# Alternating chunks of the convolution and of the projection two units ahead, on TensorE and ScalarE

## What is computed

```python
qkv = jnp.einsum('oc,bchw->bohw', w_qkv, x)                 # the projection
y = conv_general_dilated(qkv, w_dw, (1, 1), [(2, 2), (2, 2)],
                         feature_group_count=3 * INNER)     # 5x5 depthwise
agg = jnp.einsum('gok,bgkhw->bgohw', w_pw, y_grouped)        # 8x8 pointwise, by group
qkv_ms = concatenate([qkv, agg], axis=1)
# per head of 8: q, k = relu(q), relu(k); v1 = [v, 1]
vk = einsum('bhdn,bhen->bhde', v1, k)
out = einsum('bhde,bhen->bhdn', vk, q); out = out[:-1] / (out[-1:] + EPS)
out = einsum('oc,bchw->bohw', w_proj, out)                   # then batch norm, + x
```

## Time and profile before

| | |
|---|---|
| median of 3 runs | 2769.11 us (2768.99 to 2770.96) |
| the profiled execution | 2770.3 us, span 2768.5 us |
| TensorE busy | 2478.3 us, 90% of the span |
| VectorE busy | 2246.0 us, 81% |
| ScalarE busy | 870.1 us, 31% |
| mean granted TensorE clock | 0.955 of full |

### The profile page before, as it was taken

One profiled execution on the slowest core, in us unless ns is written; L12 is line 12 of the kernel. 1 busy time (PEld: TensorE's weight loads), 2 busy tenths in 40 slices (PEclk: granted clock), 3 DMA queues, 4 the chain that ended last, 5 costly groups with the idle time before them and its releaser, 6 DMA issues. The chain is left out here.

```text
span 2768.5 us, 42532 instructions
## 1 busy us (share of the span) xinstructions
PE 2478.3 (90%) x16192; PEld 1546.5 (56%) x16192; DVE 2246.0 (81%) x1677; ACT 870.1 (31%) x1685; POOL 316.9 (11%) x206
## 2 busy tenths in 40 slices
PE   7999999995998999899999999999999999999740
PEld 6888888883444554555455454555545554554420
DVE  5666666775999999899889979998997999999452
ACT  4444443442233233222323232232323233232241
POOL 2222222211000010100001010101000010100000
PEclk9999999997999999999999999999999999999975
DMA  2111110006787478477947757694776669576758
GB/s 90 69 69 69 70 69 36 35 35 191 161 181 175 103 157 206 90 169 161 217 93 161 181 118 166 137 219 98 159 181 145 136 138 217 114 160 146 246 210 372
DMA packets 89625, 397.89 MB, mean 144 GB/s; under 512 B 26480, under 2 KB 27120, under 8 KB 83696
## 3 DMA queue, kind: packets, MB, share of 16 engines
q1 hardware_dynamic: 88304, 376.43, 54.5%
q0 software_dynamic: 1152, 18.87, 1.6%
HBM read 75.12 MB, written 54.26 MB: 47 GB/s over the span
## 5 line engine op out<-in xcount | busy, mean ns | idle before, releaser
L1054 DVE SCALAR_TENSOR_TENSOR work<-work,dws 128x2304 f32<-128x2304 f32 x576 | 1511.9, 2625 | 19.5
L675 PE MATMUL cv<-work,w 128*32 128x384 f32 x6912 | 625.6, 495 | 17.8 <-ACT q L947 12.7
L653 PE MATMUL pj<-x,wqkv 128*128 128x384 f32 x1152 | 387.6, 488 | 20.4 <-DMA x<-scratch_x 20.4
L675 PEld LDWEIGHTS cv<-work,w 128*32 128x32 f32 x6912 | 195.7, 110 | 361.8 <-issue 330.0
L653 PEld LDWEIGHTS pj<-x,wqkv 128*128 128x128 f32 x1152 | 214.7, 191 | 158.6 <-issue 23.3
L680 PE MATMUL cv<-work,pwbd 128*128 128x384 f32 x576 | 266.4, 545 | 26.3 <-DVE work L1054 26.3
L897 ACT ACTIVATE work<-cv 128x384 f32<-128x384 f32 x192 | 94.5, 492 | 508.7 <-PE cv L680 508.7
L1012 POOL TENSOR_TENSOR vkm<-vkraw,mask 128x128 f32<-128x128 f32 x32 | 45.3, 1415 | 1652.5 <-ACT vkraw L917 1652.5
L872 ACT COPY work<-pj 128x384 f32<-128x384 f32 x288 | 139.0, 482 | 271.5 <-PE pj L653 243.1
L696 PE MATMUL vk<-kvT 128*128 128x129 f32 x1216 | 198.6, 286 | 8.9 <-ACT kvT L910 6.0
L680 PEld LDWEIGHTS cv<-work,pwbd 128*128 128x128 f32 x576 | 86.6, 190 | 207.8 <-issue 170.0
(11 more groups left out here) (108 smaller groups left out, 3304.6 us busy)
## 6 DMA issues: line engine op xcount, KB each, us to landing
work<-work SPq DMA_DIRECT2D x1536, 169.0 KB, 3.7
x<-scratch_x SPq DMA_DIRECT2D x9, 2304.0 KB, 10.5
scratch_x<-xs SPq DMA_DIRECT2D x8, 2304.0 KB, 7.2
xs<-in_x SPq DMA_DIRECT2D x7, 2304.0 KB, 8.6
scratch_y<-q SPq DMA_DIRECT2D x21, 768.0 KB, 3.8
work<-scratch_y SPq DMA_DIRECT2D x5, 2304.0 KB, 29.5
out<-work POOLq DMA_DIRECT2D x5, 2304.0 KB, 14.5
work<-scratch_x SPq DMA_DIRECT2D x4, 2304.0 KB, 32.0
```

The lines of the kernel that those rows point to most:

```text
L653: mm = nc.tensor.matmul(pj[:, c % 2, :CHUNK], wqkv[:, kc, u, :], x1[:, kc, c * CHUNK:(c + 1) * CHUNK], start=(kc == 0), stop=(kc == CT - 1))
L675: nc.tensor.matmul(cv[32 * b:32 * b + 32, c % 2, :CHUNK], w4[:, 4 * u + b, dy, :], taps[:, row + dy:row + dy + 8, 0:W], start=(dy == 0), s ...
L1054: op = nc.vector.scalar_tensor_tensor(out=a, in0=src, scalar=w, in1=a, op0=ALU.mult, op1=ALU.add)
```

## The change

In `image` of TensorE (L809) and of ScalarE (L957), for every unit but unit 2, a chunk of the projection two units ahead is issued right after the chunk of the convolution with the same number, inside the first loop of the unit. In the second loop it is left for unit 2 only. No instruction is added or removed, and no wait is changed; SyncE, GpSimd and VectorE keep their queues.

```diff
@@ TensorE, and the same in ScalarE @@
                     for c in range(NCH):
                         convolve(i, u, [c])
+                        if u != 2 and (u + 2 < NU or nxt):
+                            project(*unit_at(i, u + 2), [c])
                         if u == 2:
                             product(i, 2, shares(DG)[c])
                         if u == 5:
                             product(i, 3, shares(AG)[c])
                     if u == 4:
                         turn_product(i, 2)
                     for c in range(NCH):
-                        if u + 2 < NU or nxt:
+                        if u == 2:
                             project(*unit_at(i, u + 2), [c])
                         if u == 1:
                             product(i, 1, shares(AG)[c])
```

## The result

| | before | after |
|---|---|---|
| median | 2770.03 us (4 runs, 2768.99 to 2775.0) | 2907.9 us (4 runs, 2903.09 to 2912.76) |
| ratio to before | | 1.0494, 95% interval 1.0472 to 1.0516 |
| span of the profiled execution | 2768.5 us | 2911.0 us |
| mean granted TensorE clock | 0.955 | 0.935 |

The change makes the kernel 4.9% slower. The page still shows both large engines' busy time nearly unchanged: what has grown is waiting.

What follows compares the result with a forecast made beforehand. TensorE, by its own queue, was taken to bound the looped images. Terms of 20.2 us per looped image, 121 us for six, plus 14 in image 0, made 135 us: 2905 on the profiled 2770.3, median 2904, range 2848 to 2938.

Steps and rivals of the forecast that it cites:

- The bound: Looped images: TensorE's own queue sets the pace; its idling is paid in full, what reaches VectorE earlier is worth nothing.
- The alternation is free: Units 0, 1, 3, 4 and 5: convolution, projection, convolution costs 4.21 us, the same as the two apart.
- Product 1: Unit 1: loses its cover, only the first group's copy, some 0.3 us, can't be hidden; taken as 0, -0.2 to +0.5.
- `x1` in unit 4: Unit 4: TensorE's projection waits for the next image's input, 7.7 us, grown to 9.0 us, between 7.5 and 10.5.
- the tail of the `rep` loads: Unit 4: these loads land until some 39.5 us and delay `x1` by up to 1.9 us of shared transfer.
- The clock: Behind each of the two new TensorE waits, coming back from half clock costs 2.1 us (1.7 to 2.6).
- The end of unit 4: `turn_product` loses the projection ahead of it; waiting for ScalarE's copy, with the transpose, costs 0.85 us.
- half 0 of `rep`: Start of unit 5: this load is just in time for ScalarE's chunk 0 of the projection, 0.1 us.
- ScalarE's wait in unit 5: ScalarE's projection chunk 0 waits for half 1 of `rep`; TensorE idles 4.7 us, with backlog about 5.0 (3.5 to 6).
- The end of unit 5: `turn_product` waits for GpSimd's mask of the last product, which the projection covered before: 1.05 us.
- Image 0: First image, with slack for some of the loss: 5.4 us, and unit 5 adds 8.2, 14 us in all.
- The sum: 20.2 us per looped image, 121 us for images 1 to 6, with image 0 together 135 us.

Runs made afterwards that it cites:

- e1: The changed kernel with chunks alternating in units 0, 1 and 3 alone, units 4 and 5 as before: 2772.93 us, 1.0015 of the kernel before.
- e2: The changed kernel with chunks alternating in unit 4 alone: 2847.68 us, 1.0282 of the kernel before.
- e5: The changed kernel with ScalarE waiting for half 1 of `rep` only ahead of chunk 2, not chunk 0: 2860.04 us, 1.0334 of the kernel before.
- e4: The changed kernel with SyncE's load of the next `x1` moved between the two halves of unit 4's `rep` loads: 2871.44 us, 1.0371 of the kernel before.
- e6: The changed kernel with both `x1` loaded sooner and ScalarE's wait for `rep` split: 2826.77 us, 1.0214 of the kernel before.
- e9: As e6, but ScalarE itself issues the store of output chunks 4 and 5: 2807.86 us, 1.014 of the kernel before.
- e7: The kernel before with TensorE's loop over images 1 to 6 written out: 2740.45 us, 0.9907 of the kernel before.
- e3: The changed kernel with chunks alternating in unit 5 alone: 2809.3 us, 1.0143 of the kernel before.

## Why the prediction was right

The forecast was 2904 us, the measured median 2907.9. By its own steps:

- **The bound.** TensorE sets the pace, and VectorE's readiness is worth nothing: right. TensorE waits for no tap in any looped image, before or after, and what is new in its waits is paid in full.
- **The alternation is free:** right, 4.21 us per pair in e1. The Trainium skill's rule in "TensorEngine Tiling (Array Packing)", Key Properties, that a change of tiling mode drains TensorE, can't be told apart from its absence here, since the count of changes is the same in both orders.
- **Product 1:** taken at 0, range to 0.5; measured 0.7 per image, outside that range. Of it 0.42 us is the wait for the first group's copy (I had said 0.3); the rest is spread over the groups, a few hundredths each.
- **`x1` in unit 4:** 9.0 us forecast, 7.4 to 8.9 measured, 7.9 on average. Right mechanism. I had given the tail of the `rep` loads 1.3 us; comparing 7.9 with the 6.6 of e2, where unit 3 doesn't alternate, gives the shared tail this very 1.3, though no run varied the tail alone. It was the base of 7.7 us that was too high: I had taken the median landing of 10.5 us, and in e2 TensorE resumes 9.56 us after the issue (1594.85 to 1604.41).
- **The clock:** 2.1 us for each wait, and too low. The 2.07 of the image shown is near it by chance. In the six looped images the pair that resumes behind `x1` takes 5.93 to 7.30 us against 4.21, which is 1.7 to 3.1 us and 2.5 on average; in e2 it is 2.6. Behind the wait of unit 5, TensorE goes from chunk 1 to chunk 3 in 11.13 us where it doesn't wait (e5) and in 16.9 to 18.6 in the changed kernel. Less its waits, that leaves 1.6 to 3.1 us, 2.4 on average.
- **The end of unit 4:** 0.85 forecast, and 0.1 for half 0 of `rep`. What unit 4 of the image shown has grown by beside the wait and the clock is 12.15 - 8.93 - 2.07 = 1.15. Unit 4 as a whole: 12.05 forecast, 12.15 measured in that image, 11.65 on average.
- **ScalarE's wait in unit 5:** 5.0 forecast, 4.2 to 4.6 measured, 4.4 on average. The landing of half 1 was derived at 12.5 us into unit 5, and ScalarE's copy starts 12.68 us into it (1664.62 to 1677.30).
- **The end of unit 5:** 1.05 forecast; L730 starts 1.59 us behind the last group, so 1.04.
- Unit 5 up to the denominators was forecast at 8.15 us and measured at 8.79, 8.22 on average; 0.7 of the 8.79 is the loop's gap, which grew from 4.1 to 4.8 us and which I had taken as fixed. Why it grew is open.
- **Image 0:** 14 forecast, 15.6 measured. (Its first part comes out at 865.0 - 857.28 - 2.4 = 5.3, not 5.4.)

The sum was 135 us against 142.5 in the profiled executions. Of the 7.5 that are missing, 2.8 lie outside the seven images (1.8 of them ahead of the layer, where nothing was changed), 1.6 in image 0, and 3.0 in the six looped images, 20.7 each where I had 20.2. These 20.2 are nearer than their terms. Product 1 (0.7 us), the loop's gap (0.5 on average) and the clock behind the two waits (0.4 and 0.3) were too low, the wait for `x1` (1.1) and the one of unit 5 (0.6) too high. The mechanism was right; that the sum came within 3% of an image's loss is partly luck, since the errors cancel.

What failed were expectations behind it, those of e4 and e6 and, by half, that of e9: in e4 I had moved a transfer in SyncE's queue and counted what the move brings to the one who waits for it, but not who waits for what stands behind it. e2's was too low for a like reason: I had checked `rep` against chunk 0 of unit 5 and not against chunk 3.

## What to carry to other kernels

When work is moved forward in an engine's queue, its first instruction's waits move with it: list for each what must have landed, when it does, and how far back the old place stood. Here the projection's old place was 17.5 us into the unit and the input landed after 10.5; its new one was 2.8. Alternation with a lag of three chunks in the two units concerned lost 0.2%. And a wait that guards a whole buffer is often needed for a part of it only: split by rows, an edit of a few lines gave some 44 us back (ratio 1.0334 instead of 1.0494). Before a transfer is moved in a queue, list also who waits for the transfers behind it: in e4 that took back half of the gain.

## What was not expected of the hardware

- The jump back of TensorE's hardware loop costs 4.0 to 4.6 us of idle TensorE in each turn before, up to 5.1 in the other kernels, and some 1.4 us lost at the half clock behind it: 5.65 us per image in all (247.0 to 241.35). In one image of the kernel before the granted clock is 0.50 from 1631 to 1637, and the first denominators (L751, 1632.98) take 2.81 us, where they take 1.52 in e7 at a granted clock of 1.00. That the gap is due to the loop is shown by e7; why it takes this long is not tested.
- The granted clock fell from 1.00 to 0.50 in an idle stretch of 2.9 us (e3), and was still at 0.50 between 1627.00 and 1628.00, with TensorE busy since 1622.06. Behind the six waits of e3, 2.65 to 3.0 us long, TensorE lost another 1.7 to 3.2 us, 2.0 on average (from chunk 1 to chunk 3 of unit 5, against the 11.13 us of e5). The prediction had only the wait of 5.09 us in rows 7 to go by.
- GpSimd's small multiplications are slower while VectorE works. The 128x64 one behind the mask (L1014, L1018 after the change) took 2.60 to 2.62 us each of the 31 times that it ran beside one of VectorE's taps before, and 0.29 us the one time that it didn't. After the change it runs beside a tap 17 times (2.60 to 2.61 us) and without one 15 times (0.29 us), since VectorE waits more. The mask ahead of it (L1012) is less regular: 0.45 us with VectorE idle, 0.46 to 2.9 us beside a tap. The Trainium skill, in "SBUF — State Buffer", Who interferes with whom, describes a port pair that VectorE and GpSimd share and lock. The trace agrees with it in direction; no run here tested the cause.
